# A vision tower with two attention layers and two expert stages: router and low-rank rows from turned h, and a prologue that rounds further ahead

## The reference

```python
h = tower(x)      # conv 14x14 into patches, 9 windows of 9 patches, local and class attention
h = h + attention0(layernorm(h))        # 16 heads over the 10 tokens
xn = layernorm(h)
logits = xn @ router_w                  # 256 -> 8, top 2, softmax over the two
h = h + moe(xn)                         # 8 experts 256 -> 1024 -> 256, gelu, norm of (xn + out), gates
h = h + attention1(layernorm(h))        # causal, scores clipped to +-10
x = layernorm(h)
gate = softmax(x @ router_W.T + router_b); sparse = renormalized top 2 of 6
h = h + x @ base_W.T + base_b + low_rank(x, sparse)   # ranks of 16: one shared, six routed
```

## Time and profile before

| | us |
|---|---|
| median of 3 runs (lowest, highest) | 821.78 (821.37, 822.71) |
| profiled execution, its time | 819.8 |
| its span, first to last instruction | 817.7 |
| PE busy | 716.3 (88%) |
| DVE busy | 508.0 (62%) |
| POOL busy | 414.1 (51%) |
| ACT busy | 374.7 (46%) |
| mean granted PE clock | 0.941 |

### The profile page before, as it was taken

How to read it: one execution, slowest core, us unless ns; L and a number is a source line. 1 busy time by engine, 2 the same in 40 slices (tenths; PEclk the granted TensorE clock), 3 DMA queues, 4 the chain that set the end, 5 groups by cost and what they waited for, 6 DMA issues and landing times.

```text
span 817.7 us, 12959 instructions
## 1 busy us (share of the span) xinstructions
PE 716.3 (88%) x4311; PEld 616.5 (75%) x4311; DVE 508.0 (62%) x1233; ACT 374.7 (46%) x935; POOL 414.1 (51%) x279
## 2 busy tenths in 40 slices
PE   3979999999999999999808755999999999495978
PEld 3869998988989898655607645999999999353866
DVE  3668787778778677769799561222222222588956
ACT  3555565656556555533131422444444444165251
POOL 3755757677575761348849602433333432226820
PEclk9989999999999999999967956999999999699899
DMA  8642223212312120000020065889988881400001
GB/s 260 189 131 66 69 90 89 73 62 89 90 56 79 45 79 25 1 1 0 1 104 1 37 264 215 322 321 309 341 332 336 328 308 71 166 6 1 1 1 64
DMA packets 34487, 102.73 MB, mean 126 GB/s; under 512 B 3624, under 2 KB 12152, under 8 KB 27000
## 3 DMA queue, kind: packets, MB, share of 16 engines
q1 hardware_dynamic: 31832, 94.84, 33.5%
q0 software_dynamic: 2592, 7.10, 2.3%
HBM read 95.75 MB, written 6.17 MB: 125 GB/s over the span
## 4 chain that ended last, share of the span: by engine, by line
PE 73%; POOL 9%; DVE 9%; issue 2%; DMA 2%; ACT 2%; POOLq 1%; SPq 0%; DVEq 0%; ACTq 0%
PE banks L1631 12%; PE banks L1639 11%; PE banks L287 10%; PE banks L289 10%; PE banks L288 10%; PE banks L294 6%; PE banks L300 4%; POOL a_prod L1155 3%; PE banks L1285 2%; POOL a_prod L1170 2%; PE banks L1315 2%; POOLq L282 1%; PE banks L1969 1%; DVE banks L1438 1%; POOL rstd L336 1%
## 5 line engine op out<-in xcount | busy, mean ns | idle before, releaser
L401 POOL TENSOR_TENSOR x_lo<-xraw,x_hi 128x640 fp32r<-128x640 f32 x81 | 128.5, 1594 | 105.1 <-ACT x_hi L395 105.1
L287 PE MATMUL banks<-wc_hi,x_hi 128*128 128x256 f32 x405 | 120.6, 298 | 14.2 <-POOL x_lo L401 14.1
L1729 ACT ACTIVATE hid<-banks,b 128x128 f32<-128x128 f32 x216 | 79.3, 367 | 109.9 <-PE banks L1631 109.9
L288 PE MATMUL banks<-wc_lo,x_hi 128*128 128x256 f32 x405 | 115.7, 286 | 0.0
L289 PE MATMUL banks<-wc_hi,x_lo 128*128 128x256 f32 x405 | 115.6, 286 | 0.0
L287 PEld LDWEIGHTS banks<-wc_hi,x_hi 128*128 128x128 f32 x405 | 78.4, 194 | 16.3 <-issue 14.8
L1888 DVE TENSOR_TENSOR res<-banks,xb 128x256 f32<-128x256 f32 x27 | 11.5, 424 | 127.1 <-PE banks L1639 127.1
L288 PEld LDWEIGHTS banks<-wc_lo,x_hi 128*128 128x128 f32 x405 | 78.5, 194 | 1.8 <-issue 0.2
L424 DVE BATCH_NORM_STATS2 stats<-banks 128x6 f32<-128x256 f32 x81 | 34.7, 428 | 71.8 <-ACT pe_sb L418 71.1
L418 ACT ACTIVATE pe_sb<-banks 128x256 f32<-128x256 f32 x81 | 31.0, 383 | 105.4 <-PE banks L289 105.4
L289 PEld LDWEIGHTS banks<-wc_hi,x_lo 128*128 128x128 f32 x405 | 78.4, 194 | 0.0
(11 more groups left out here) (306 smaller groups left out, 1707.2 us busy)
## 6 DMA issues: line engine op xcount, KB each, us to landing
w_raw<-in_w SPq DMA_DIRECT2D x28, 1024.0 KB, 6.7
xraw<-in_x_main SPq DMA_DIRECT2D x27, 768.0 KB
w1more<-in_w SPq DMA_DIRECT2D x13, 1024.0 KB, 5.6
w2more<-in_w SPq DMA_DIRECT2D x13, 1024.0 KB, 8.2
xraw<-in_x_rest SPq DMA_DIRECT2D x27, 114.0 KB
yl<-y_rows SPq DMA_DIRECT2D x2, 1028.0 KB, 7.0
a_w<-in_qkv_w SPq DMA_DIRECT2D x2, 768.0 KB, 5.4
x_rows<-w_raw SPq DMA_DIRECT2D x5, 256.0 KB, 2.0
```

Of the source, the lines that this page charges most:

```text
L287: pe.matmul(dst, a[0], b[0], start=start, stop=False)
L288: pe.matmul(dst, a[0], b[1], start=False, stop=False)
L401: pool.tensor_tensor(x_lo[:, i % RING_X, :], xraw[:, k].rearrange("p c b -> p (c b)"), x_hi[:, i % RING_X, :], ALU.subtract).then_inc(sem( ...
L1729: act.activation(hid[:, s % 2, fc, :], bank(fc % 2, 0, P), ACT.Gelu, bias=b1[:, bass.ds(e * FC + fc, 1)]).then_inc(sem("gelu_made"), 1)
```

## The change

```diff
-            pool_scores(pool, 0, 6, T)
+            pool_scores(pool, 0, 7, T)
 
         def dve_end(dve, link):
             weigh(dve, link, NW - 1)
...
@@ -1332,11 +1337,24 @@
                     pe.matmul(bank(6 + t % 2), a_oT[:, t % 2, c * P:(c + 1) * P], wo[:, c, :], start=(c == 0), stop=False)
                 pe.matmul(bank(6 + t % 2), ident[:, :], h_at(t), start=False, stop=True).then_inc(sem("a_o_done"), 1)
 
+            if layer == 0:
+                pe_router_sums(pe)
             for t in range(T):
                 turn_o(t)
                 if t:
                     project_o(t - 1)
+                if layer == 0 and t >= 3:
+                    turn_h(pe, t - 3)
+                if layer == 0 and t >= 4:
+                    logits(pe, t - 4)
+                if layer == 1 and t == T - 3:
+                    pe_lora_rows(pe, 0)
             project_o(T - 1)
+            if layer == 0:
+                for t in range(T - 3, T):
+                    turn_h(pe, t)
+                    logits(pe, t - 1)
+                logits(pe, T - 1)
...
                 if t:
                     copy_h(act, layer, t - 1)
+                if layer == 0 and t >= 3:
+                    copy_hT(act, t - 3)
                 if layer == 0 and t == 7:
                     norm_rows(act, 0)
+                if layer == 1 and t == T - 3:
+                    act_lora_rows(act, 0)
...
+        def lower_half(dve, g):
+
+            s_g = half_scores(a_s, 0, g)
+            dve.tensor_tensor(s_g, s_g, top_bank(g).unsqueeze(3).broadcast_to([P, HALF, H16, T]), ALU.subtract)\
+               .then_inc(sem("a_s_made"), 1)
...
             dve.tensor_tensor(share(p_g, pooled), share(p_g, pooled), scales(pooled), ALU.mult).then_inc(sem("a_p_made"), 1)
+            if layer == 0 and g == 0:
+                lower_half(dve, 1)
...
                         row_scores(dve, link, 1, t)
-                    if t == T - 1:
+                    if t == T - 2:
                         softmax_half(dve, link, 1, 0)
...
-                for g in range(2):
-                    s_g = half_scores(a_s, 0, g)
-                    max_g = a_max[:, g * HALF * H16:(g + 1) * HALF * H16].rearrange("p (t h) -> p t h", t=HALF)
-                    link(dve.tensor_reduce(max_g, s_g, AX, ALU.max))
-                    dve.tensor_tensor(s_g, s_g, max_g.unsqueeze(3).broadcast_to([P, HALF, H16, T]), ALU.subtract)\
-                       .then_inc(sem("a_s_made"), 1)
-                for g in range(2):
-                    softmax_half(dve, link, 0, g)
+                link(dve.tensor_reduce(top_bank(0), half_scores(a_s, 0, 0), AX, ALU.max))
+                lower_half(dve, 0)
+                link(dve.tensor_reduce(top_bank(1), half_scores(a_s, 0, 1), AX, ALU.max))
+                softmax_half(dve, link, 0, 0)
...
+                if layer == 0 and t == HALF:
+                    softmax_half(dve, link, 0, 1)
+                if layer == 0 and i == 1:
+                    center_router(dve)
...
             for t in range(added, T):
                 add_o(dve, layer, t)
-            following, ends, parts = after(layer)
-            shift_of(dve, *batch_of(following, parts - 1))
+                if layer == 0 and t == T - 2:
+                    route_top(dve, link, *GROUPS[0])
...
+        def pe_router_sums(pe):
+            pe.wait_ge(sem("moe_small_loaded"), 32)
+            pe.wait_ge(sem("route_consts"), 1)
+            for c in range(CH):
+                last = pe.matmul(bank(5, 0, E), ones[:, :], w_rt[:, c, :], start=(c == 0), stop=(c == CH - 1))
+            last.then_inc(sem("route_summed"), 1)
+
+        def center_router(dve):
+            dve.wait_ge(sem("route_summed"), 1)
+            for c in range(CH):
+                dve.scalar_tensor_tensor(out=w_rt[:, c, :], in0=bank(5, 0, E), scalar=-1.0 / C, in1=w_rt[:, c, :],
+                                         op0=ALU.mult, op1=ALU.add).then_inc(sem("route_ready"), 1)
+
+        def turn_h(pe, t):
+            pe.wait_ge(sem("a_h_made"), t + 1)
+            if t == 0:
+                pe.wait_ge(sem("route_ready"), CH)
+            else:
+                pe.wait_ge(sem("hT_made"), min(t, GROUPS[2][0]))
+            turn(pe, turned_bank(t), h_at(t)).then_inc(sem("h_turned"), 1)
+
+        def logits(pe, t):
+            pe.wait_ge(sem("hT_made"), t + 1)
+            mm_rows(pe, logits_at(t, t + 1), hT[:, t % 4, :], w_rt, 0, E).then_inc(sem("lg_done"), 1)
+
+        def copy_hT(act, t):
+            act.wait_ge(sem("h_turned"), t + 1)
+            if t >= 4:
+                act.wait_ge(sem("lg_done"), t - 3)
+            act.activation(hT[:, t % 4, :], turned_bank(t), ACT.Copy).then_inc(sem("hT_made"), 1)
...
+            pe.wait_ge(sem("z_loaded"), 64)
+            for c in range(CH):
+                last = pe.matmul(bank(5, 0, ZW + C), ones[:, :], z_w[:, c, :], start=(c == 0), stop=(c == CH - 1))
+            last.then_inc(sem("z_summed"), 1)
...
+            shift_of(dve, *batch_of("experts", 2))
+            link(dve.tensor_tensor(tw[:, :, :], top[:, :, 0:2], top[:, :, 0:1].broadcast_to([P, T, 2]), ALU.subtract))
+            dve.tensor_tensor(tw[:, :, :], tw[:, :, :], rstd[1][:, :].unsqueeze(2).broadcast_to([P, T, 2]), ALU.mult)\
                .then_inc(sem("tw_made"), 1)
...
+            dve.wait_ge(sem("z_loaded"), 64)
+            dve.wait_ge(sem("z_summed"), 1)
+            for c in range(CH):
+                dve.scalar_tensor_tensor(out=z_w[:, c, :], in0=bank(5, 0, ZW + C), scalar=-1.0 / C, in1=z_w[:, c, :],
+                                         op0=ALU.mult, op1=ALU.add)
...
+        def z_bank(g):
+            a, b = GROUPS[g]
+            return bank((2, 3, 2)[g], 0, (b - a) * ZW)
+        def pe_lora_rows(pe, g):
+            a, b = GROUPS[g]
+            def turn_z(t):
+                pe.wait_ge(sem("a_h_made"), seen(1, "h_made", t + 1))
+                if t >= 2:
+                    pe.wait_ge(sem("z_hT_made"), t - 1)
+                turn(pe, bank(4 + t % 2), h_at(t)).then_inc(sem("z_turned"), 1)
+
+            def z_rows_of(t):
+                pe.wait_ge(sem("z_hT_made"), t + 1)
+                if t == GROUPS[2][0]:
+                    pe.wait_ge(sem("z_made"), 1)
+                mm_rows(pe, z_bank(g)[:, (t - a) * ZW:(t - a + 1) * ZW], z_hT[:, t, :], z_w, 0, ZW).then_inc(sem("z_done"), 1)
+
+            for t in range(a, b):
+                turn_z(t)
+                if t > a:
+                    z_rows_of(t - 1)
+            z_rows_of(b - 1)
+
+        def act_lora_rows(act, g):
+            a, b = GROUPS[g]
+            for t in range(a, b):
+                act.wait_ge(sem("z_turned"), t + 1)
+                act.activation(z_hT[:, t, :], bank(4 + t % 2), ACT.Copy).then_inc(sem("z_hT_made"), 1)
+            act.wait_ge(sem("z_done"), b)
+            act.activation(z[:, a:b, :], z_bank(g).rearrange("p (t n) -> p t n", t=b - a), ACT.Copy).then_inc(sem("z_made"), 1)
...
+            pe_lora_rows(pe, 1)
+            pe_lora_rows(pe, 2)
+            pe.wait_ge(sem("z_hT_made"), T)
...
+            dve.wait_ge(sem("z_turned"), 8)
+            link(dve.tensor_tensor(h_at(0, 8).rearrange("p (t c) -> p t c", t=8), h_at(0, 8).rearrange("p (t c) -> p t c", t=8),
+                                   z_rows[:, 0:C].unsqueeze(1).broadcast_to([P, 8, C]), ALU.add))
+            dve.wait_ge(sem("z_turned"), T)
+            link(dve.tensor_tensor(h_at(8, 2).rearrange("p (t c) -> p t c", t=2), h_at(8, 2).rearrange("p (t c) -> p t c", t=2),
+                                   z_rows[:, 0:C].unsqueeze(1).broadcast_to([P, 2, C]), ALU.add))
+            dve.wait_ge(sem("z_made"), 3)
+            dve.wait_ge(sem("rstd_made"), batch_of("low rank", 1)[0] + 1)
             over = lambda x, n: x[:, :].unsqueeze(2).broadcast_to([P, T, n])
+            link(dve.tensor_tensor(z_l[:, :, :], z[:, :, LOW:ZW], over(rstd[1], E6), ALU.mult))
...
-            dve.wait_ge(sem("z_h_made"), T)
-            for t in range(0, T, 2):
-                dve.wait_ge(sem("z_out_done"), t + 2)
-                dve.tensor_tensor(z_o[:, t:t + 2, :], out_bank(t, 2), h_at(t, 2), ALU.add).then_inc(sem("z_out_made"), 1)
+            for t in range(T):
+                dve.wait_ge(sem("z_out_done"), t + 1 + (t + 1) % 2)
+                dve.scalar_tensor_tensor(out=h_at(t), in0=out_bank(t), scalar=rstd[1][:, t:t + 1], in1=h_at(t),
+                                         op0=ALU.mult, op1=ALU.add).then_inc(sem("z_out_made"), 1)
...
             sp_experts(sp)
+            sp.dma_start(z_w[:, :, 0:ZW], two("z_w")).then_inc(sem("z_loaded"), 16)
+            sp.dma_start(z_w[:, :, ZW:ZW + C], two("base_w")).then_inc(sem("z_loaded"), 16)
+            sp.dma_start(z_b[:, :], d["z_b"]).then_inc(sem("z_loaded"), 16)
+            sp.dma_start(z_rows[:, :], d["z_rows"].broadcast_to([P, C + E6])).then_inc(sem("z_loaded"), 16)
             phase(sp, 2)
             sp_combine(sp)
```

(26 more changed lines are left out.)

173 lines of the change are left out of this document (57 added, 116 removed).

## The result

| | before | after |
|---|---|---|
| median of 4 runs (lowest, highest) | 821.75 (821.37, 822.71) | 810.84 (807.13, 811.26) |
| ratio, 95% interval | | 0.985 [0.982, 0.988] |
| profiled execution | 819.8 | 807.13 |
| its span | 817.7 | 805.4 |

The change makes the kernel 10.9 us (1.5%) faster; 20.35 were forecast, and the range ended at 807.0. In a second set of five runs the changed kernel had 809.44 (807.12 to 811.63).

A forecast was written before the change was run, and what follows sets the result against it. PE was taken to bound the kernel (73% of the chain), its windows and experts unchanged. Terms summed to -20.35 us: 819.8 profiled to 799.45, plus 2.0 for the median, 801.4; 8-in-10 range 796.5 to 807.

The forecast's parts named there:

- 1, prologue: Before PE's first `wkv_hi` matmul: with copies four patches ahead, POOL's waits for ACT go; -4.3 us, bounds -6 and -1.5.
- B: Prologue: POOL's splits without gaps hold up DVE's variances and shifts, eating the gain; 804.3 to 805.6 us; chance 0.14.
- 2: Score products: job 6 fills POOL's wait for the class token's variance, ending DVE's later idling; -2.9 us.
- 3: Softmax: the second half's subtraction no longer stands in front of the first sum; -0.85 us.
- 4, routing: Routing: only turn, copy and logits now follow h of token 9, so the last logits come sooner; -6.8 us.
- Rival E: PE's turns of h in the outputs' loop wait for ACT's copies behind `a_oT` copies; 806 us; chance 0.05.
- Rival C: Routing: the first gather lands late, behind the first weights' burst; 6.35 us lost, 807.8; chance 0.10.
- 5: End of the experts: column sums of `z_w` and DVE's centrings before phase 2 delay SP's row loads; +2.9 us.
- 6, attention 1: Attention 1: softmax one step sooner starts POOL's values 2.66 us sooner, partly offset by four tiles' inserted rows; -0.8 us.
- 7: Low-rank stage: only six tiles' turns and rows stand between last output and first base matmul; -7.6 us.

## Why the prediction was wrong, step by step

- **1, prologue: the step that failed first.** "Four patches ahead these waits go" took it for granted that the input is there. The row that said otherwise was the input itself: SP issues the load of patches 9 to 11 behind eight other loads, and in the prologue before it was just in time, because ACT came late: behind the copy that ends at 30.99, ACT rounds patch 9 at 31.09, and with the new order, where ACT is ready for it at 27.5, at 30.95. With the inputs ahead the first matmul came at 41.36, against 42.3 forecast. The list of rivals had POOL and DVE holding each other up (B), which changed nothing, and not the DMA. The row of the kernel before:

```profile
31.09 0.74 ACT L395 ACTIVATE x_hi<-xraw 128x640 fp32r<-128x640 f32 x1
```

- **2, 3:** right in mechanism and in size (2.7 and 0.75 for 2.9 and 0.85).
- **4, routing:** mechanism right, the term mis-sized: the way from the last fold grew by 2.4, not 1.0. 1.2 of it is ACT's normalizing of `x2`, which the sum did not place in ACT's list at all. Before, this block started 1.2 behind the fold, as soon as POOL's power and DVE's shift were there; now it starts 3.2 behind it, though POOL's power ends at 455.7, because DVE's shift comes only at 457.8: DVE's list was held by the instruction of 3.76 that the last section shows. That this delay is what made the block cost anything is an estimate from these rows; no run tests it. Rival E named ACT's list, but for the copies. Rival C did not come: the gather, issued 10.7 sooner, was followed by PE's start after 6.4 instead of 6.7. The block in the kernel before:

```profile
461.55 2.07 ACT L364 ACTIVATE w_raw<-h,nmr,rstd 128x256 f32<-128x256 f32 x4 [3.05 <-DVE nmr L341]
```

- **Experts: -1.0 that no term had.** The first slot runs at half the clock longer, 487.7 to 494 against 498.7 to 503. It is not the change's doing: from the turn of the first slot to that of the third it is 11.59 before and 12.58 in the changed kernel, but 11.55 to 12.69 in the other profiles, whose slots are the same. Why the clock returns sooner or later is open.
- **5:** 2.55 for 2.9, and avoidable in the main. The size was right by luck. The row of 3.49 for a projection is not at full clock, as the forecast says: the granted clock there is 0.55, and rows at full clock take 1.98 for the same four matmuls. And the two products stand in the trace as four of 374 columns, not two. Too high a price on too few columns gave 2.55; at the right ones it would be 1.45 at full clock and 2.9 at half, and 2.86 were measured. The row at full clock, from the kernel before:

```profile
377.63 1.98 PE L1285 MATMUL banks<-a_w,a_xT 128*128 128x512 f32 x4
```

- **6, attention 1: the second step that failed.** The difference of starts on POOL (2.66 forecast, 2.67 measured behind the loads) was taken through to the end, though PE's first projection needs ACT's copy, and that stands behind the exponent of token 9. PE's first projection is 54.5 behind the loads in both kernels. The four tiles of rows cost 1.7 there, near the 1.87 of the sum. The other 0.7 goes with the clock, which was down for longer behind PE's new wait. Rows of the kernel before show the order in ACT's list:

```profile
759.64 0.49 ACT L1372 ACTIVATE a_p<-a_s 128x160 f32<-128x160 f32 x1 [4.57 <-DVE a_s L1433]
759.92 0.84 ACT L1407 ACTIVATE a_oT<-banks 128x256 f32<-128x256 f32 x2
```

- **7:** 7.2 for 7.6. DVE's gating stayed 0.9 in front of its need.
- **Median over profile:** the changed kernel's profile was the shortest run of its set; its median lies 3.7 above, where 2.0 were taken over from the kernel before.

## What to carry to other kernels

When an engine is allowed to run ahead, look up when its input lands, not only who held it back: the slack that the old order left hides a transfer that is just in time. A buffer made earlier is worth what the next reader's queue allows, so walk the whole list of every engine between it and the bound, and count optional work that stands in it (here four tiles of `x2` and one exponent). New idle time on PE in front of dense work can cost more than its length, since the matmuls behind it may run at 1.2 instead of 2.4 GHz for some microseconds: 1.6 us were lost so in front of the windows.

## What the runs showed that I had not expected

- The same kernel has PE's clock up or down behind the same wait of 2.80 (7.91 and 9.47 for the same matmuls). Each such episode is 1.6 us, and executions of one kernel differ by one or two of them.
- One instruction of DVE on four elements a row took 3.76 beside POOL's product, until that product ended (447.99 + 3.76 = 451.75; POOL's product ends at 451.73), and 3.67 to 4.00 in all other profiles with the changed order. Its like before took 1.02. The Trainium skill ("Advanced Engine Details and Errata", VectorE Performance Modes) states that GpSimd and VectorE's two-port instructions block each other; the trace agrees in that end. DVE's shift, for which ACT waited 3.92 in front of its normalizing, stands behind it in DVE's list; what that cost was not tested. The instruction in the changed kernel, and its like before:

```profile
447.99 3.76 DVE L350 TENSOR_SCALAR veps<-mv 128x4 f32<-128x4 f32 x1
...
451.65 1.02 DVE L354 TENSOR_SCALAR veps<-mv 128x4 f32<-128x4 f32 x1
```
